# A graph attention pair with its per-head order of work changed: normalisation by bank, maxima further ahead, the q chain on GpSimd, a_src rows from bfloat16 parts, h in quarters

## The chip, the cores and the metric

One core of a Trainium2 chip runs the whole program. The metric is the device time of one execution in microseconds (us). Three runs of the kernel before took 1505.25, 1492.67 and 1501.57 us, so the median is 1501.57 us. The profile is one further execution.

## The reference

`x` is 1024 nodes by 512 features. A graph layer, a mixture of experts, a graph attention pair and a second mixture of experts each add their result to `x`. The change is in the attention pair alone. `src` and `dst` hold 17,408 edges of the same graph. For each of the two layers (8 heads, 128 channels per head in the first, 64 in the second):

```
h = (x @ W).reshape(N, heads, out_ch)
a_src = einsum('nhc,hc->nh', h, att_src);  a_dst = einsum('nhc,hc->nh', h, att_dst)
e = leaky_relu(a_src[src] + a_dst[dst], 0.2)
m = segment_max(e, dst);  ex = exp(e - m[dst]);  s = segment_sum(ex, dst)
out = segment_sum(h[src] * (ex / (s[dst] + 1e-16)), dst) + bias
```

Layer 1 is followed by relu, layer 2 by a log_softmax over its 512 features.

## The kernel before

The graph is dense in this kernel: `CT` holds, for every pair of source (partition) and destination (free axis), the logarithm of how many edges there are, and `mask` (bfloat16) a large number where there is no edge. `attend` (line 1268) runs twice, "a1" for layer 1 and "a2" (`final`) for layer 2. A **pair** is one head and one tile of 128 source nodes: 8 heads x 8 tiles = 64 pairs, numbered k, with head hd = k // 8 and tile s = k % 8. Each engine has its own in-order program and the programs meet at semaphores.

For every pair: GpSimd adds `CT` and the q row of the head (`qb`) into `am` (L1339, a ring of 4); ScalarE writes the relu of a_dst + a_src into PSUM banks 4 and 5 (L1350, one buffer, so relu of pair k+1 waits until VectorE has added pair k); VectorE adds the two (`counted`, L1438); ScalarE takes the exponential into `PT` (L1357, a ring of 4; ScalarE's order is relu k+1, then exp k); TensorE multiplies `PT` with `h`. In layer 1 this is `gather` (L1536): 8 matmuls of 129 columns (128 channels and a column of ones that gives the sum s), for 8 destination tiles in 3 PSUM banks (PER = 3 tiles a bank, NBK = 3), opened by 3 matmuls on zeros (L1532) once VectorE has emptied the banks. In layer 2 it is `columns` (L1547): two matmuls of 512 columns with the result transposed in banks 0 and 1, which ScalarE copies out once a head (`moved`, L1364, at s = 1 of the next head), TensorE turns back (`rows`, L1558, at s = 2) and VectorE divides (`normed`, at s = 4).

`normed` (L1440 to L1459) divides a head's sums. In layer 1 it comes at s = 1 of the next head and reads all three banks with one instruction; TensorE turns the result (`turned`, L1568, at s = 3 and 7) and ScalarE moves it to x2T (`out`, L1368, at s = 6 and s = 1).

The q row of a head needs the maximum of a_src over the neighbours of each node. `a_row` (L1517) has TensorE broadcast row a_src of the head to all partitions in banks 6 and 7, from the float32 tile `aTs`; `maxed` (L1422) takes 8 masked maxima on VectorE from it; `q` (L1425 to L1433) makes four instructions of 8 columns from these; SP then writes q4 to memory (L1319), waits for it, and loads it as a broadcast `qb` (L1321). The maxima of heads 0 and 1 are taken before the first pair. Those of head hd + 2 are taken in head hd, the last one and q at s = 0 of the next.

`h` comes as 16 units (`h_tile`, L1523), one per node tile and half of the heads. The 8 units of the first half are made before the first pair, the 8 of the second between gathers, by the table H_AFTER (3, 2, 2 and 1 of them in heads 0 to 3), all through bank 3; ScalarE moves them to `h` (`h_moved`, L1373) by the table H_MOVED. `turned` and `rows` use bank 3 too, so they wait for the moving of each unit in front of them.

## Time and profile before

| | |
|---|---|
| median of 3 runs | 1501.57 us (1492.67 to 1505.25) |
| profiled execution, own time | 1511.43 us, span 1509.7 us |
| TensorE matmul busy | 1096.2 us (73%) |
| VectorE busy | 950.1 us (63%) |
| ScalarE busy | 607.4 us (40%) |
| GpSimd busy | 581.9 us (39%) |
| mean granted TensorE clock | 0.844 |
| attention layer 1 | from 806.7 to 1057.6 us of the span |
| attention layer 2 | from 1057.6 to about 1350 us of the span |

A busy share is a mean over the whole program. The attention pair has to be read from its own stretch, head by head: where an engine sat idle, and what released it. In a timeline row the first number is the start in us from the span's start, the second the length, then the engine, the line, the operation, the tiles, how many records are merged, and in brackets the idle time in front of it with its releaser. A float32 matmul leaves two records, so 16 records of L1536 are one gather.

### The profile page before, as it was taken

The page shows a single profiled execution, that of the slowest core. Times are in us where ns is not written, and L with a number is a line of the kernel's source. Part 1 is how long each engine was busy: PE and PEld are TensorE (multiplying, and loading weights), DVE is VectorE, ACT ScalarE, POOL GpSimd, SP SyncE. Part 2 cuts the span into 40 slices and gives each one's busy share as a digit, 9 for nine tenths or more (in the row PEclk, how much of TensorE's full clock was granted, in tenths as well). Part 3 has the DMA queues.
Part 4 walks back from the last instruction along what each step waited for, and adds up shares of the span by engine and source line. Part 5 has one row for each costly group of instructions (what it writes and reads, how often), then busy time and mean ns, then how long its engine had stood idle before and what let it go on. Part 6 is the DMA issues. An engine that isn't in the chain of part 4 may idle for free. (4 is left out here: it accounts for less than half of the span.)

```text
span 1509.7 us, 18794 instructions
## 1 busy us (share of the span) xinstructions
PE 1096.2 (73%) x5288; PEld 754.5 (50%) x5292; DVE 950.1 (63%) x1829; ACT 607.4 (40%) x835; POOL 581.9 (39%) x493
## 2 busy tenths in 40 slices
PE   3788768952478788778607899968999876816586
PEld 1343356741467777667303477858454421205473
DVE  6466576448345566565595689994277777464355
ACT  0322343230233343443111477767046767731231
POOL 0000044403668784000330576765066667601102
PEclk9999979965678899998758899979899988865697
DMA  2000000032488999998512111110211011001795
GB/s 87 0 0 1 0 1 0 0 122 79 151 262 276 304 299 295 298 305 280 169 40 72 42 43 29 54 32 15 72 42 43 28 49 42 14 1 36 260 322 185
DMA packets 118761, 164.20 MB, mean 109 GB/s; under 512 B 26357, under 2 KB 68925, under 8 KB 118698
## 3 DMA queue, kind: packets, MB, share of 16 engines
q1 hardware_dynamic: 101722, 124.37, 26.3%
q0 software_dynamic: 5600, 18.35, 3.8%
q10 hardware_dynamic: 11376, 20.71, 3.7%
q8 instruction: 30, 0.49, 0.1%
q14 instruction: 33, 0.27, 0.1%
HBM read 133.59 MB, written 29.82 MB: 108 GB/s over the span
## 5 line engine op out<-in xcount | busy, mean ns | idle before, releaser
L1339 POOL TENSOR_TENSOR am<-CT,qb 128x1024 f32<-128x1024 f32 x128 | 300.6, 2362 | 193.2 <-DMA qb<-q_scratch 110.3
L1438 DVE TENSOR_TENSOR am<-PS,am 128x1024 f32<-128x1024 f32 x128 | 156.6, 1223 | 53.3 <-ACT PS L1350 48.6
L1350 ACT ACTIVATE PS<-adb,ab 128x1024 f32<-128x1024 f32 x128 | 143.0, 1117 | 103.2 <-DVE am L1438 102.7
L973 PE MATMUL PS<-xgT,w1r 128*128 128x128 f32 x1264 | 179.1, 303 | 2.6 <-DMA w2r<-in_L_ffn_W 2.6
L973 PEld LDWEIGHTS PS<-xgT,w1r 128*128 128x128 f32 x1264 | 172.2, 219 | 4.1 <-DMA w2r<-in_L_ffn_W 3.4
L1422 DVE CUSTOM_DVE_ANT_0 masked<-PS,mask 128x1024 f32<-128x1024 f32 x128 | 156.1, 1220 | 27.8 <-issue 26.1
L1547 PE MATMUL PS<-PT,h 128*65 128x512 f32 x256 | 136.0, 679 | 37.3 <-ACT PT L1357 19.8
L1357 ACT ACTIVATE PT<-am,as 128x1024 f32<-128x1024 f32 x128 | 145.1, 1134 | 0.7 <-DVE am L1438 0.6
L1536 PEld LDWEIGHTS PS<-h,PT 128*128 128x128 f32 x1024 | 127.9, 206 | 11.3 <-ACT PT L1357 7.5
L1055 DVE TENSOR_TENSOR w2l<-w2r,w2h 128x1024 fp32r<-128x1024 f32 x79 | 105.6, 1337 | 43.5 <-ACT w2h L1023 42.4
L1536 PE MATMUL PS<-h,PT 128*128 128x129 f32 x1024 | 128.6, 289 | 5.5 <-ACT PT L1357 5.5
L1010 ACT ACTIVATE hT<-PS,b1T 128x128 f32<-128x128 f32 x158 | 49.5, 364 | 194.4 <-PE PS L973 126.8
L964 PE MATMUL PS<-ident,xg 128*128 128x128 f32 x316 | 56.8, 309 | 87.0 <-DMA xg<-xs_scratch 86.5
L1051 DVE COPY yo<-PS 128x512 f32<-128x512 f32 x79 | 54.5, 690 | 100.8 <-PE PS L983 82.4
L335 DVE TENSOR_SCALAR oh_src<-iota,eT 128x1024 f16 x164 | 78.8, 481 | 55.8 <-PE PS L451 45.3
L1023 ACT CAST w2h<-w2r 128x1024 fp32r<-128x1024 f32 x79 | 82.5, 1045 | 59.3 <-DMA w2r<-in_L_ffn_W 45.5
L885 POOL TENSOR_TENSOR prod<-prod 128x256 f32<-128x256 f32 (+4 forms) x176 | 94.2, 535 | 13.8
L1547 PEld LDWEIGHTS PS<-PT,h 128*65 128x65 f32 x256 | 37.2, 156 | 124.0 <-issue 61.0
L964 PEld LDWEIGHTS PS<-ident,xg 128*128 128x128 f32 x316 | 39.0, 154 | 112.3 <-DMA xg<-xs_scratch 82.4
L451 PE MATMUL PS<-oh_src,oh_dst 128*128 x328 | 78.2, 386 | 22.5 <-DVE oh_dst L337 22.5
L171 PE MATMUL PS<-ident,xln 128*128 128x128 f32 x96 | 19.7, 374 | 84.6 <-DVE xln L152 83.9
L1045 DVE COPY xgT<-PS 128x512 f32<-128x512 f32 x79 | 53.9, 682 | 37.1 <-PE PS L964 37.1
(288 smaller groups left out, 1852.4 us busy)
## 6 DMA issues: line engine op xcount, KB each, us to landing
w1r<-in_L_ffn_W SPq DMA_DIRECT2D x79, 512.0 KB, 5.3
w2r<-in_L_ffn_W SPq DMA_DIRECT2D x79, 512.0 KB, 6.9
ys_scratch<-yo ACTq DMA_DIRECT2D x79, 256.0 KB, 4.9
xg<-xs_scratch SPq DMA_DIRECT2D x71, 128.0 KB, 4.6
adb<-a_scratch SPq DMA_DIRECT2D x16, 512.0 KB, 3.7
qb<-q_scratch SPq DMA_DIRECT2D x16, 512.0 KB, 4.1
wc<-in_L_gnn_W POOLq DMA_DIRECT2D x16, 256.0 KB, 5.7
xg<-xs_scratch SPq DMA_DIRECT2D x15, 256.0 KB, 5.1
```

Of the source, the lines that this page charges most:

```text
L885: pool.tensor_tensor(to, by[:, :, 0:width], by[:, :, width:2 * width], ALU.add).then_inc(s_prod, 1)
L964: mm = pe.transpose(PS[:, j % 2, k * P:(k + 1) * P], xg[:, j, k * P:(k + 1) * P], ident[:])
L973: mm = pe.matmul(PS[:, 2 + j % 2, c * P:(c + 1) * P], w1r[:, j, k, c * P:(c + 1) * P], xgT[:, j % 2, k, :], start=(k == 0), stop=(k == KD ...
L1023: act.copy(w2h[:, j % 2, :, :], w2r[:, j, :, :]).then_inc(s_wh, 1)
L1055: dve.tensor_tensor(w2l[:, j % 2, :, :], w2r[:, j, :, :], w2h[:, j % 2, :, :].bitcast(F32), ALU.subtract).then_inc(s_wl, 1)
L1339: pool.tensor_tensor(am[:, k % RING, :], CT[:, s, :], qb[:, hd % 2, :], ALU.add).then_inc(s_sum, 1)
L1350: act.activation(RELU, adb[:, hd % 2, :], ACT.Relu, bias=ab[:, s, hd:hd + 1]).then_inc(s_relu, 1)
L1357: act.activation(PT[:, k % PR, :], am[:, k % RING, :], ACT.Exp, bias=as02[:, s, hd:hd + 1], scale=1 - NEG_SLOPE).then_inc(s_exp, 1)
L1422: dve.tensor_tensor_reduce(masked[:], ASB, mask[:, t, :], 1.0, -3.0e38, ALU.subtract, ALU.max, mrow[:, hd % 2, t:t + 1]).then_inc(s_max, 1)
L1438: dve.tensor_tensor(am[:, k % RING, :], RELU, am[:, k % RING, :], ALU.add).then_inc(s_all, 1)
L1536: mm = pe.matmul(PS[:, d // PER, (d % PER) * (CH + 1):(d % PER + 1) * (CH + 1)], PT[:, (NT * hd + s) % PR, d * P:(d + 1) * P], h[:, s, hd, ...
L1547: mm = pe.matmul(PS[0:CH + 1, half, :], h[:, s, hd, :], PT[:, (NT * hd + s) % PR, half * 512:(half + 1) * 512], start=(s == 0), stop=(s == ...
```

## The change

- `normed` in layer 1 moves from s = 1 to s = 0 of the next head and divides bank by bank with three instructions, each with its own count on s_ev. `gather` loses the three zero matmuls; its first matmul into each bank starts the bank, and waits for that bank's count.
- `moved` in layer 2 goes from s = 1 to s = 0.
- q leaves VectorE. GpSimd does it in five instructions, behind the add of pair 8(hd-1) for heads from 3 on, and behind pairs 4 and 7 for heads 1 and 2. The q row of head 0 is made by TensorE (8 broadcast matmuls, `q_row`) and a copy on ScalarE, with no trip through memory.
- 13 maxima are taken before the first pair (16 before), the rest one or two behind each add; the first of head hd + 3 at s = 7 of head hd.
- `a_row` for heads from 2 on is a bfloat16 matmul over 80 rows: `aTs` is split into three bfloat16 parts in `a3` by ScalarE copies and GpSimd subtractions before the first pair. It stands in front of the gather of s = 5, three heads ahead (from head 3 on), and waits for all maxima of the head in front.
- `h`: 6 units before the first pair, 10 later (2, 2, 2, 1, 2, 1 in heads 0 to 5). A unit of the second half is now two node tiles by two heads: twice the matmuls with half the columns.
- Every gather waits for the units it reads (`h_ready`). The adb and qb rows have semaphores of their own.

```diff
-            H_AFTER = {(0, 1): 0, (0, 3): 1, (0, 5): 2, (1, 1): 3, (1, 5): 4, (2, 1): 5, (2, 5): 6, (3, 1): 7}
-            H_MOVED = {(0, 4): 0, (0, 6): 1, (1, 0): 2, (1, 4): 3, (2, 0): 4, (2, 4): 5, (3, 0): 6, (3, 4): 7}
-            MAXED = {2: (0,), 3: (1,), 4: (2,), 5: (3,), 6: (4,), 7: (5, 6)}
+            H0 = 6
+            H_AFTER = dict(zip(((0, 1), (0, 3), (1, 1), (1, 5), (2, 1), (2, 5), (3, 5), (4, 1), (4, 5), (5, 1)),
+                               range(H0, 2 * NT)))
+            H_MOVED = {(hd + (s + 3) // NT, (s + 3) % NT): i for (hd, s), i in H_AFTER.items()}
+            EARLY = 5
+            FIRST = {0: ((1, 5),), 1: ((1, 6),), 2: ((1, 7),), 3: ((2, 0), (2, 1)), 4: ((2, 2), (2, 3)),
+                     5: ((2, 4), (2, 5)), 6: ((2, 6), (2, 7)), 7: ((3, 0),)}
+            LATER = ({0: (1,), 1: (2,), 2: (3,), 3: (4,), 5: (5, 6), 6: (7,)} if final else
+                     {1: (1,), 2: (2,), 3: (3,), 4: (4, 5), 5: (6,), 6: (7,)})
+            A_ROW = {1: 2, **{8 * (hd - 3) + 5: hd for hd in range(3, HEADS)}}
+            Q_AFTER = {4: 1, 7: 2, **{NT * (hd - 1): hd for hd in range(3, HEADS)}}
...
+                    def q(hd):
+                        pool.wait_ge(s_max, NT * hd + NT)
+                        a_dst = ab[:, :, HEADS + hd:HEADS + hd + 1].rearrange("p t o -> p (t o)")
+                        link(pool.tensor_tensor(zx[:], mrow[:, hd % 2, :], a_dst, ALU.add), 4 * hd + 1)
+                        link(pool.tensor_scalar(zy[:], zx[:], 0.0, SLOPE - 1, ALU.max, ALU.mult), 4 * hd + 2)
+                        link(pool.tensor_tensor(zx[:], zx[:], zy[:], ALU.add), 4 * hd + 3)
+                        link(pool.tensor_tensor(zx[:], a_dst, zx[:], ALU.subtract), 4 * hd + 4)
+                        wait(pool, s_qrow, 16 * (hd - 2))
+                        pool.tensor_scalar(q4[:, hd % 2, :], zx[:], 1 / (SLOPE - 1), None, ALU.mult).then_inc(s_q, 1)
...
+                    pool.wait_ge(s_high, 1)
+                    pool.tensor_tensor(rest[:], aTs[:], a3[0:2 * HEADS, :], ALU.subtract).then_inc(s_rest, 1)
+                    pool.wait_ge(s_mid, 1)
+                    pool.tensor_tensor(rest[:], rest[:], mid[:], ALU.subtract).then_inc(s_last, 1)
...
+                    for i in range(2, H0 - 2):
+                        h_moved(i, i % 2)
+                    act.wait_ge(s_q0, 1)
+                    act.copy(qb[:, 0, :], PS[:, 2:4, :].rearrange("p a n -> p (a n)")).then_inc(s_q0m, 1)
...
                     relu(0)
+                    for i in range(H0 - 2, H0):
+                        h_moved(i, i % 2)
...
-                        if final and s == 1 and hd:
+                        if final and s == 0 and hd:
                             moved(hd - 1)
...
-                        if s == 0 and hd and hd + 1 < HEADS:
-                            maxed(hd + 1, NT - 1)
-                            q(hd + 1)
-                        if hd and s == (4 if final else 1):
+                        if hd and s == (4 if final else 0):
                             normed(hd - 1)
-                        if hd + 2 < HEADS:
-                            for t in MAXED.get(s, ()):
-                                maxed(hd + 2, t)
+                        for ahead, t in maxima(hd, s):
+                            maxed(ahead, t)
...
                     def a_row(hd):
                         wait(pe, s_max, NT * hd)
+                        if hd >= 2:
+                            pe.wait_ge(s_a3, 1)
+                            for half in range(2):
+                                mm = pe.matmul(PS[:, 6 + half, :], sel[0:A3, hd:hd + 1].to_broadcast([A3, P]),
+                                               a3[0:A3, half * 512:(half + 1) * 512], start=True, stop=True)
+                            mm.then_inc(s_as, 1)
+                            return
...
                     def gather(hd, s):
-                        if s == 0:
-                            wait(pe, s_ev, hd)
-                            for b in range(NBK):
-                                pe.matmul(PS[:, b, 0:PER * (CH + 1)], onesb[:], zerob[:, 0:PER * (CH + 1)],
-                                          start=True, stop=False)
+                        h_ready(hd, s)
                         pe.wait_ge(s_exp, NT * hd + s + 1)
                         for d in range(NT):
+                            if s == 0 and d % PER == 0:
+                                wait(pe, s_ev, NBK * (hd - 1) + d // PER + 1)
...
-                        if s == 0 and hd + 2 < HEADS:
-                            a_row(hd + 2)
+                        if k in A_ROW:
+                            a_row(A_ROW[k])
                         columns(hd, s) if final else gather(hd, s)
```

## Rows read from the trace of the kernel before

**Rows 1.** Head 1, layer 1, by windows: us, busy PE, PEld, DVE, ACT, POOL, PEclk, DMA.

```profile
910.00:936.00 26.00, 25.40 (x161) 19.17 (x159) 25.16 (x40) 19.14 (x21) 18.77 (x8) 1.00 0.14 42
```

**Rows 2.** TensorE's timeline in layer 1.

```profile
857.34 5.92 PE L1536 MATMUL PS<-h,PT 128*128 128x129 f32 x32 [4.75 <-ACT PT L1357]
...
870.11 3.60 PE L1523 MATMUL PS<-W1t,xT 128*128 128x512 f32 x8
...
880.55 3.73 PE L1536 MATMUL PS<-h,PT 128*128 128x129 f32 x32
...
981.50 1.98 PE L1517 MATMUL PS<-aTs,ident 16*128 16x512 f32 x4
989.25 1.15 PE L1532 MATMUL PS<-zerob,onesb 128*128 128x387 bf16 x3 [5.77 <-DVE o L1458]
...
1045.07 7.39 PE L1536 MATMUL PS<-h,PT 128*128 128x129 f32 x64
```

**Rows 3.** VectorE's timeline at the head ends of layer 1.

```profile
981.38 2.27 DVE L1429 TENSOR_TENSOR zx<-mrow,ab 128x8 f32<-128x8 f32 x1
...
986.25 1.22 DVE L1438 TENSOR_TENSOR am<-PS,am 128x1024 f32<-128x1024 f32 x1
...
987.83 1.36 DVE L1458 TENSOR_TENSOR o<-PS,rd 128x1152 f32<-128x1152 f32 x1
989.11 1.21 DVE L1438 TENSOR_TENSOR am<-PS,am 128x1024 f32<-128x1024 f32 x1
...
991.58 1.23 DVE L1438 TENSOR_TENSOR am<-PS,am 128x1024 f32<-128x1024 f32 x1
...
1001.50 1.22 DVE L1438 TENSOR_TENSOR am<-PS,am 128x1024 f32<-128x1024 f32 x1
...
1005.06 1.22 DVE L1438 TENSOR_TENSOR am<-PS,am 128x1024 f32<-128x1024 f32 x1
```

**Rows 4.** ScalarE's timeline in front of the first pairs of layer 1.

```profile
833.04 0.59 ACT L1373 COPY h<-PS 128x512 f32<-128x512 f32 x1 [2.85 <-PE PS L1523]
...
856.14 1.15 ACT L1357 ACTIVATE PT<-am,as 128x1024 f32<-128x1024 f32 x1
```

**Rows 5.** SP's timeline in layer 1, two issues of head 1.

```profile
852.57 0.37 SPq L1319 DMA_DIRECT2D q_scratch<-q  x1
862.13 0.32 SPq L1321 DMA_DIRECT2D qb<-q_scratch  x1
```

**Rows 6.** VectorE, ScalarE and TensorE by timeline, layer 2, where head 4 begins.

```profile
1221.76 1.22 DVE L1438 TENSOR_TENSOR am<-PS,am 128x1024 f32<-128x1024 f32 x1
...
1224.07 1.13 ACT L1357 ACTIVATE PT<-am,as 128x1024 f32<-128x1024 f32 x1
...
1228.20 0.99 ACT L1364 COPY a_oT<-PS 65x1024 f32<-65x1024 f32 x1
...
1236.67 0.66 PE L1558 MATMUL PS<-ident,a_oT 65*128 65x65 f32 x8
1237.16 3.60 PE L1547 MATMUL PS<-PT,h 128*65 128x512 f32 x8
```

**Rows 7.** Other places of layer 2 by timeline, TensorE and VectorE.

```profile
1243.05 7.06 PE L1547 MATMUL PS<-PT,h 128*65 128x512 f32 x12 [2.29 <-ACT PT L1357]
...
1306.65 8.14 PE L1547 MATMUL PS<-PT,h 128*65 128x512 f32 x12 [3.93 <-ACT a_oT L1364]
...
1154.38 0.17 DVE L1447 TENSOR_SCALAR dn<-PS 128x8 f32<-128x8 f32 x1 [4.39 <-PE PS L1558]
...
1315.32 0.17 DVE L1447 TENSOR_SCALAR dn<-PS 128x8 f32<-128x8 f32 x1 [3.90 <-PE PS L1558]
```

**Rows 8.** A stretch of layer 2 by windows: us, PE busy, PEclk, DMA share, GB/s.

```profile
1244.00:1247.70 3.70, 3.70 (x6) 0.54 0.00 0
```

**Rows 9.** GpSimd: line 1339 by source, and one group by form.

```profile
L1339 POOL TENSOR_TENSOR am<-CT,qb x128: 2337/2362/2397, 842.8 to 1311.2; 128x1024 f32<-128x1024 f32 x128
...
L885 POOL TENSOR_TENSOR prod<-prod 128x8 f32<-128x8 f32 x16 | 5.9, 370 | 1.3
```

More of the change, by code:

```diff
@@ L1315, in _ @@
                             sp.wait_ge(s_exp, NT * (hd - 1))
-                        sp.dma_start(adb[:, hd % 2, :], bcast(adr[HEADS + hd], N)).then_inc(s_in[hd % 2], 16)
-                        sp.wait_ge(s_q, hd + 1)
-                        with nc.allow_non_contiguous_dma(reason="one value per tile and partition"):
-                            sp.dma_start(qdr[hd].rearrange("(t p) -> p t", p=P), q4[:, hd % 2, :]).then_inc(s_qrow, 16)
-                        sp.wait_ge(s_qrow, 16 * (hd + 1))
@@ L1321, in _ @@
-                        sp.dma_start(qb[:, hd % 2, :], bcast(qdr[hd], N)).then_inc(s_in[hd % 2], 16)
-                        if final and hd == 4:
+                        sp.dma_start(adb[:, hd % 2, :], bcast(adr[HEADS + hd], N)).then_inc(s_ad[hd % 2], 16)
+                        if hd:
+                            sp.wait_ge(s_q, hd + 1)
+                            with nc.allow_non_contiguous_dma(reason="one value per tile and partition"):
+                                sp.dma_start(qdr[hd].rearrange("(t p) -> p t", p=P), q4[:, hd % 2, :]
+                                             ).then_inc(s_qrow, 16)
+                            sp.wait_ge(s_qrow, 16 * hd)
+                            sp.dma_start(qb[:, hd % 2, :], bcast(qdr[hd], N)).then_inc(s_qb[hd % 2], 16)
@@ L1554, in rows @@
                         wait(pe, s_ev, hd)
-                        wait(pe, s_hm, NT + moved)
+                        wait(pe, s_hm, moved)
                         for d in range(NT):
@@ L1569, in turned, with q_row @@
                         mm.then_inc(s_tr, 1)
+                    def q_row(hd):
+                        pe.wait_ge(s_q, hd + 1)
+                        pe.wait_ge(s_bm, 1)
+                        for t in range(NT):
+                            mm = pe.matmul(PS[:, 2 + t // 4, (t % 4) * P:(t % 4 + 1) * P],
+                                           q4[:, hd % 2, t:t + 1].to_broadcast([P, P]), ident[:], start=True, stop=True)
+                        mm.then_inc(s_q0, 1)
                     a_row(0)
                     pe.wait_ge(s_w[0], 16)
-                    for t in range(NT):
-                        wait(pe, s_hm, t - 1)
-                        h_tile(0, t, t % 2)
-                        if t == 4:
+                    for i in range(H0):
+                        wait(pe, s_hm, i - 1)
+                        h_tile(i, i % 2)
+                        if i == H0 - 3:
                             a_row(1)
+                            q_row(0)
                     pe.wait_ge(s_w[1], 16)
-                    pe.wait_ge(s_hm, NT)
+                    pe.wait_ge(s_hm, H0)
+                    pe.wait_ge(s_q0m, 1)
                     pe.wait_ge(s_ones, 1)
-                    pe.wait_ge(s_bm, 1)
                     turns = 0
@@ L1601, in _ @@
                     if final:
[L1602 removed]
+                        rows(HEADS - 1, 2 * NT)
                     else:
[L1604 to L1605 removed]
+                        turned(HEADS - 1, 0, 2 * NT)
+                        turned(HEADS - 1, 1, 2 * NT)
         phase()
```

139 lines of the change are left out of this document (97 added, 42 removed).

## The prediction, made before the changed kernel was built or run

> **What bounds the kernel now.** I read the page first. Its forty slices show no engine full throughout, so the attention pair had to be read head by head. Windows over layer 1 came next: head 1 has TensorE busy 25.40 of 26.00 us, at the full granted clock [rows 1]. Heads 0 to 2 are bound by TensorE. TensorE's timeline shows what changes later: from head 3 on it sits idle at the head's end, 5.77 us in one case, until VectorE has divided [rows 2]. VectorE's timeline says why: q starts at 981.38 and the next add comes only at 986.25, so four instructions of 8 columns took 4.87 us [rows 3]. They have SBUF tiles alone as inputs, and GpSimd's 2.36 us adds run beside them [rows 9]; adds with one side in PSUM kept 1.22 us there. In layer 2 TensorE waits instead for ScalarE's copy `moved`, and VectorE then for the rows turned back [rows 6, 7].
>
> **Prices used.** A layer-1 gather takes 3.73/2 = 1.87 us at the full clock, a unit of h 3.43, a float32 a_row about 1.95 [rows 2]. Adds follow each other every 2.48 us with one maximum between them, 3.56 us with two; an exponential ends 3.45 us after its add began (1224.07 + 1.13 - 1221.76) [rows 3, 6]. A layer-2 pair on TensorE takes 1.80 us, turning back 0.5 [rows 6]. The bfloat16 a_row has no row; between 0 and the 1.95 us of the float32 one I take 0.45, since one zero matmul of 387 bfloat16 columns took at most 1.15/3 = 0.38. Three banks divided singly have no row either: between the 1.36 us of the one instruction and three times that, I take 1.5, since the work is the same 1152 columns. A unit of second-half h in layer 2 becomes 16 matmuls of 128 columns, like two gathers: 3.74 us against 3.45.
>
> An idle gap also costs clock. After 4.75 us of idle two gathers took 5.92 instead of 3.73, 2.2 us more [rows 2]; after 2.29 us the mean granted clock of 3.7 us was 0.54, nearly all of it at the lower level of 1.2 GHz, so 3.7 x 0.46 = 1.7 us were lost [rows 7, 8]. Between 0 and 2.2 us a gap I take 1.75. The Trainium skill (TensorE: Matmul & The Clock Gate, Part 1) puts the ramp penalty at under 1% of a typical kernel's span and warns against modelling it by a count. By it the clock terms below fall away and the sum would be -19.5 us instead of -4.
>
> **Start of layer 1.** The fourth unit of h is done at 833.0 [rows 4]. Then come a_row(1) 1.95, q_row (8 matmuls of 128 columns, like a gather) 1.7 to 1.9, ScalarE's copy 1.0 and relu 1.1. Units 4 and 5 end at 843.5 and their copy at 844.1; relu and the exponential with its table load take 3.6 more, so the first gather starts at 847.7. It was 857.34 [rows 2]. The a3 copies fit in ScalarE's gaps of 2.85 us [rows 4]; without them they would cost some 3 us. Head 0 then has two units instead of three, but VectorE, which has 11 maxima left to fit in behind its adds, holds a_row(3) to about 866. Its last gather ends at 872.5, against 880.55 + 3.73 = 884.3: **-11.8**.
>
> **Heads 1 to 7 of layer 1.** Let 0 be the end of the last gather of the head before. VectorE, which has added pair 0 already, is now held at `normed` until exactly this moment; before, q and one more add covered that wait. The first bank is divided at 1.05, so gather 0 runs to 2.95. All three are done at 1.95; add 1 follows, its exponential ends at 5.4, and TensorE idles 2.5 us. Gather 1 to 7.3, unit to 10.8, gathers 2 and 3, a turn and gather 4 to 17.0, with the clock price 18.7. Adds run at 1.95, 4.4, 6.9, 9.4, 13.0, 15.4, so the head's last maximum is in at 17.9. a_row waits for it, and gather 5 behind a_row. Then 0.45, gather 5, a unit, gathers 6 and 7: 18.7 + 0.45 + 3 x 1.87 + 3.43 = 28.2. Heads 1, 2 and 4 take this. Head 3 has no early unit, so TensorE idles about 3 us in front of a_row: 17.9 + 9.5 + 1.75 = 29.2. Head 5 has no a_row and ends with its last exponential, 23.4; heads 6 and 7 with no maxima 22.3 each. The sum is 181.8. Before it was 1052.46 - 884.3 = 168.2 [rows 2]: **+13.6**. The removed zero matmuls and q are in this; their cover is gone with them.
>
> **Start of layer 2.** The same steps bring the first pair 8.4 us forward. `moved` now follows the exponential of s = 0: it begins 3.45 us after add 0, where it began 6.4 after (1228.20 - 1221.76) [rows 6]. `rows` is held by the move of the unit behind s = 1 at s = 4, and head 1 still starts at the low clock. Head 0's division comes at 1147.3 instead of 1154.4 [rows 7]: **-7.1**.
>
> **Heads 1 to 7 of layer 2.** Let 0 be the start of add 0. `moved` ends at 4.4, which delays relu 2 and so add 2 to 5.5; adds 3 and 4 start at 8.0 and 10.4. The unit behind s = 1 can be moved at 14.3 only, behind the exponential of s = 4, so `rows` ends and the division begins at 14.9 (11.7 where there is no such unit). Adds 5 and 6 start at 16.0 and 19.6, and the last maximum is in at 22.1. a_row waits for it; behind it stand 0.45, three pairs of 1.80, a unit of 3.74 and the clock, 11.5 us together, so the head's last pair ends at 33.7 and `moved` at 34.7. VectorE alone would begin the next head at 24.6 and allow `moved` to end at 29.0. The head thus takes 24.6 + 5.7 = 30.2: heads 2 and 4. Head 1, which starts behind a gap, has its first three pairs slow, 1.5 us more at the division: 31.7. Head 3 has no early unit, 3.2 less: 27.1. Head 5 has no a_row: 24.6. Head 6 has no maxima, 20.2, and starts behind a gap of 1.7: 21.7. Head 7's division stands 13.1 after its add 0, head 1's 16.4. That makes 165.5 + 13.1 - 16.4 = 162.2 between the divisions of heads 0 and 6, against 1315.3 - 1154.4 = 160.9: **+1.3**. From there to the end nothing changes; the bias load now follows the last qb and lands long before the log_softmax needs it.
>
> **GpSimd and SP.** The five instructions of q have between 0 and 5 x 2.36 = 11.8 us, the length of five whole adds; the nearest row has 8 columns in 0.37 us [rows 9], so I take 2 us with the waits between them. q(hd) stands between pairs 0 and 1 of head hd - 1 in GpSimd's queue, and begins when the last maximum is in. From there add 1 of the next head leaves it 9 us in layer 1's heads with a late unit and 5 in head 5. Layer 2 leaves 2 to 3 us before add 1 itself is late, but in heads 1 to 4 add 2 waits for `moved` far longer. So it costs nothing; at the upper end it would cost 3 to 7 us in most heads. q4's way through memory takes 9.56 us [rows 5], then the load, for which I allow 4; it stands behind adb in SP's queue, and the tightest case, head 7 of layer 2, has 2.5 us to spare. Nothing for it either.
>
> **Sum.** -11.8 + 13.6 - 7.1 + 1.3 = -4.0 us. The profiled execution took 1511.43 us with a span of 1509.7, so it would come to 1507.4. It lies 9.9 above the median; I apply the difference to the median: 1501.57 - 4 = **1497.6 us**.
>
> **Rivals.** *Clock stays up (faster).* The gap at a head's start is cut in two by gather 0, and the gap in front of a_row can come out shorter than 2.29 us. Then 1.75 goes four times in layer 1 where 0.7 (three heads) and 1.75 (head 3) was exposed (-4), and in layer 2 four times behind a_row and three times in front of the division (-11.4): 1501.57 - 19.5 = 1482. For it: head 1 of layer 1 never left the full clock [rows 1], and by the sum above TensorE stays busy 23 of a head's 28 us. Against it: 2.29 us was enough [rows 7, 8]. Chance 0.26.
>
> *TensorE starts cold twice a head (slower).* Place: heads 1 to 4 of both layers, at the division and behind a_row, where now two gaps stand instead of one. In one row three pairs took 8.14 instead of 5.4 us after a gap [rows 7], 2.7 each. Twice 2.7 less the 1.75 counted is 3.65 a head, 8 heads, +29: 1527. It decides once a head's two gaps cost over 4.2 us, where the time passes 1% above the median. Against it: VectorE's waits hide part of the first one. Chance 0.12. The Trainium skill (TensorE: Matmul & The Clock Gate, HAM oscillation) describes a loop in which every turn's gap brings the clock down anew; by it the time is this rival's.
>
> *The wait at `normed` is not there (faster).* If VectorE were never held, heads would run at its own 21.9 and the change would win over 25 us, 1475. Against it: the last gather ends 1.9 us behind its exponential, and the add of pair 0 ends before that. Chance 0.05. *q or its row comes late*, or the change acts nowhere: 0.02, same range as the forecast.
>
> **The numbers.** The forecast has 0.55 with its own range of 1488 to 1507, from the bounds of the clock and of the three-bank division (8 heads x 1 us). To hold 8 in 10 the range takes in the first rival and leaves out the second: 1477 to 1513. One per cent, about what a measurement tells from no change, is 15 us. Faster by over 1% (below 1486.6): 0.29, from the two fast rivals and a tail. Slower by over 1%: 0.12. Within: 0.59.
>
> **What would show it.** Right: the first gather of layer 1 near 848; VectorE idle in front of `normed` in layer 1 for 1 to 6 us, released by TensorE; heads 1 to 4 of layer 1 at 27 to 29 us and longer than before; heads 6 and 7 at 22; TensorE waiting at a_row for a maximum; clock 0.50 behind it. Wrong: heads of layer 1 under 25 us, no wait of VectorE for the last gather, GpSimd's q over 5 us, or qb as the releaser of adds.

## The result: 0.7% faster, inside the forecast

| | before | changed |
|---|---|---|
| median | 1499.22 us (20 runs, 1489.08 to 1505.25) | 1488.14 us (20 runs, 1474.25 to 1495.73) |
| profiled execution, own time | 1511.43 us | 1485.29 us |
| span | 1509.7 us | 1483.0 us |
| ratio of the times | | 0.993, interval 0.9904 to 0.9955 |

The change gains 11.1 us where I had forecast 4.0 with 1477 to 1513 around it. It is less than the 1% that I had set as the bound of "the same", but outside the measurement's own uncertainty. The median of the kernel before is now 1499.22 us over 20 runs, where the forecast started from 1501.57 over 3.

The two profiled spans lie 26.7 us apart, more than the medians do; the profiled execution of the kernel before was slower than each of its 20 timed runs. To see which part belongs to the change I cut each span at three places that both traces have: the first matmul of a_src and a_dst of layer 1, that of layer 2, and the first statistics of the normalisation behind the attention. All times in this table are differences of such starts.

| us | before | changed | difference |
|---|---|---|---|
| ahead of the attention (code unchanged) | 806.79 | 791.84 | -15.0 |
| layer 1 | 250.88 | 252.25 | +1.4 |
| of it, to the end of head 0's last gather | 77.5 | 67.0 | -10.5 |
| of it, heads 1 to 7 | 168.2 | 179.0 | +10.8 |
| layer 2 | 294.29 | 279.47 | -14.8 |
| of it, to the division of head 0 | 96.7 | 85.6 | -11.1 |
| of it, divisions of heads 0 to 6 | 160.95 | 158.09 | -2.9 |
| behind the attention (code unchanged) | 157.74 | 159.44 | +1.7 |

The attention and what follows it differ by 11.8 us, about the medians' 11.1. The 15 us ahead of it lie in code that neither kernel changes. In the eleven other profiles of this study that stretch took 788 to 802 us, so one profile says little about it, and I count none of it for the change. The same spread bounds every reading below: identical code of layer 2 took 279.5, 279.7 and 276.3 us in three kernels, identical code of layer 1 252.3 and 255.4. The starts of the layers hold in all of them: 65.4 to 68.9 us for head 0 of layer 1 in the eight kernels that share the changed code there (77.5 and 78.1 with the old code), 83.9 to 88.5 us in layer 2 (96.7 and 97.6).

### The profile page after: what moved, and what is told of

It is laid out like the page before. It is cut to its first block and busy times, and to the rows that moved or that the text cites. A ratio compares the mean times of both kernels' runs of the same rounds, so it can differ in the third digit from the quotient of the medians.

```text
span 1483.0 us, 19362 instructions
## 1 busy us (share of the span) xinstructions
PE 1057.4 (71%) x5468; PEld 743.3 (50%) x5468; DVE 908.0 (61%) x1781; ACT 614.4 (41%) x845; POOL 609.9 (41%) x587
## 5 line engine op out<-in xcount | busy, mean ns | idle before, releaser
L973 PE MATMUL PS<-xgT,w1r 128*128 128x128 f32 x1264 | 165.1, 287 | 3.4 <-DVE xgT L1045 1.8
L973 PEld LDWEIGHTS PS<-xgT,w1r 128*128 128x128 f32 x1264 | 157.3, 203 | 6.3 <-issue 3.0
L1647 PE MATMUL PS<-PT,h 128*65 128x512 f32 x256 | 125.6, 623 | 23.9 <-ACT PT L1427 14.1
L964 PE MATMUL PS<-ident,xg 128*128 128x128 f32 x316 | 53.1, 293 | 80.0 <-DMA xg<-xs_scratch 79.8
L451 PE MATMUL PS<-oh_src,oh_dst 128*128 x328 | 78.9, 389 | 22.0 <-DVE oh_dst L337 21.9
L964 PEld LDWEIGHTS PS<-ident,xg 128*128 128x128 f32 x316 | 35.7, 145 | 107.9 <-DMA xg<-xs_scratch 87.7
L1647 PEld LDWEIGHTS PS<-PT,h 128*65 128x65 f32 x256 | 33.5, 142 | 97.6 <-issue 80.8
L1178 POOL DMA_INDIRECT yb<-ys_scratch,r_posi x16 | 16.4, 1023 | 142.7 <-POOLq L1085 138.2
```

Source lines behind the costliest of these rows:

```text
L964: mm = pe.transpose(PS[:, j % 2, k * P:(k + 1) * P], xg[:, j, k * P:(k + 1) * P], ident[:])
L973: mm = pe.matmul(PS[:, 2 + j % 2, c * P:(c + 1) * P], w1r[:, j, k, c * P:(c + 1) * P], xgT[:, j % 2, k, :], start=(k == 0), stop=(k == KD ...
L1647: mm = pe.matmul(PS[0:CH + 1, half, :], h[:, s, hd, :], PT[:, (NT * hd + s) % PR, half * 512:(half + 1) * 512], start=(s == 0), stop=(s == ...
```

## The profile after

The head of the page of the changed kernel: busy time and share of each engine, then the costliest groups of instructions, with their idle time in front and its releaser.

```profile
PE 1057.4 (71%) x5468; PEld 743.3 (50%) x5468; DVE 908.0 (61%) x1781; ACT 614.4 (41%) x845; POOL 609.9 (41%) x587
...
L1407 POOL TENSOR_TENSOR am<-CT,qb 128x1024 f32<-128x1024 f32 x128 | 299.3, 2363 | 61.5 <-ACT PT L1427 39.5
L1520 DVE TENSOR_TENSOR am<-PS,am 128x1024 f32<-128x1024 f32 x128 | 156.6, 1223 | 77.2 <-ACT PS L1420 67.7
```

VectorE lost 42 us of work and TensorE 39 us, and the time moved by 11. That is what a busy share can't tell. Now stretches of layer 1 by windows, from division to division: first head 1 of the kernel before, then heads 1 and 2 of the changed kernel; then, in each of the two heads, what follows the gap ahead of the gather of s = 1; the last window lies in layer 2 behind an a_row. The columns are those of [rows 1].

```profile
884.32:909.23 24.91, 24.91 (x160) 19.35 (x161) 24.07 (x40) 17.21 (x18) 18.79 (x8) 1.00 0.13 43
...
858.80:886.00 27.20, 22.70 (x169) 21.39 (x169) 20.78 (x37) 19.95 (x20) 25.16 (x16) 1.00 0.15 40
886.00:914.10 28.10, 24.67 (x173) 22.94 (x172) 20.78 (x37) 19.49 (x20) 20.15 (x14) 0.94 0.15 39
...
864.29:868.00 3.71, 3.71 (x25) 3.50 (x26) 3.61 (x8) 3.27 (x4) 3.71 (x3) 1.00 0.03 4
891.93:898.80 6.87, 6.87 (x32) 6.11 (x33) 6.45 (x14) 6.29 (x7) 6.47 (x3) 0.75 0.26 76
...
1137.60:1141.20 3.60, 3.60 (x6) 1.23 (x5) 3.44 (x7) 2.96 (x4) 3.43 (x5) 0.50 0.02 5
```

In head 1 of the kernel before TensorE was busy for all of 24.91 us. Here it is busy for 22.70 of 27.20: head 1 has less work for it and takes longer. The window of [rows 1], which I called head 1, is head 2 by the divisions (909.23 to 935.47 us); it went from 25.40 of 26.00 us to 24.67 of 28.10. TensorE's timeline shows where it stands, first around the division of head 0, then in head 3 of layer 1:

```profile
854.75 4.07 PE L1634 MATMUL PS<-h,PT 128*128 128x129 f32 x35
860.01 2.02 PE L1634 MATMUL PS<-h,PT 128*128 128x129 f32 x16 [1.20 <-DVE o L1545]
864.29 2.02 PE L1634 MATMUL PS<-h,PT 128*128 128x129 f32 x16 [2.26 <-ACT PT L1427]
...
932.15 0.60 PE L1602 MATMUL PS<-a,sel 80*128 80x512 bf16 x2 [2.86 <-DVE mrow L1514]
932.60 1.95 PE L1634 MATMUL PS<-h,PT 128*128 128x129 f32 x16
934.38 3.62 PE L1619 MATMUL PS<-W1t,xT 128*128 128x256 f32 x16
```

VectorE's timeline at the same division, in order. It waits for the last gather, divides three banks, and only then comes the add of pair 1:

```profile
856.38 1.23 DVE L1520 TENSOR_TENSOR am<-PS,am 128x1024 f32<-128x1024 f32 x1 [1.59 <-POOL am L1407]
858.86 0.17 DVE L1529 TENSOR_SCALAR dn<-PS 128x9 f32<-128x9 f32 x1 [1.25 <-PE PS L1634]
859.06 0.22 DVE L1531 RECIPROCAL rd<-dn 128x9 f32<-128x9 f32 x1
859.31 1.49 DVE L1545 TENSOR_TENSOR o<-PS,rd 128x384 f32<-128x384 f32 x3
860.71 1.22 DVE L1520 TENSOR_TENSOR am<-PS,am 128x1024 f32<-128x1024 f32 x1
```

This wait of VectorE is in all eight heads of layer 1; its group of instructions puts 31.6 us on TensorE's gather (3.74 of them behind head 7, where nothing is held up by it), and 19.3 us on the turned rows of layer 2:

```profile
L1529 DVE TENSOR_SCALAR dn<-PS 128x9 f32<-128x9 f32 (+1 forms) x16 | 2.6, 166 | 50.9 <-PE PS L1634 31.6 <-PE PS L1658 19.3
```

In layer 2, head 1, TensorE waits for the maximum, falls to the lower of its two clock levels (0.50 granted, 1.2 GHz, window 1137.60 above), and stands again for `moved`. The last two rows are the a_row of head 3, where the pair behind a wait of 2.98 us ran at its full speed:

```profile
1136.76 1.04 PE L1602 MATMUL PS<-a,sel 80*128 80x512 bf16 x2 [3.63 <-DVE mrow L1514]
1137.59 3.62 PE L1647 MATMUL PS<-PT,h 128*65 128x512 f32 x4
1141.00 4.47 PE L1619 MATMUL PS<-W2t,x2T 128*128 128x128 f32 x32
1145.30 3.60 PE L1647 MATMUL PS<-PT,h 128*65 128x512 f32 x8
1150.00 1.93 PE L1647 MATMUL PS<-PT,h 128*65 128x512 f32 x4 [1.10 <-ACT a_oT L1434]
...
1195.48 0.60 PE L1602 MATMUL PS<-a,sel 80*128 80x512 bf16 x2 [2.98 <-DVE mrow L1514]
1195.92 1.88 PE L1647 MATMUL PS<-PT,h 128*65 128x512 f32 x4
```

q, which took VectorE 4.87 us in [rows 3] (two instructions of 2.27 us and two of 0.17), takes GpSimd 1.5 us from its first to its last instruction, here for head 0 and in every head behind it:

```profile
813.87 0.21 POOL L1379 TENSOR_TENSOR zx<-mrow,ab 128x8 f32<-128x8 f32 x1 [0.70 <-DVE mrow L1514]
814.17 0.27 POOL L1380 TENSOR_SCALAR zy<-zx 128x8 f32<-128x8 f32 x1
814.53 0.20 POOL L1381 TENSOR_TENSOR zx<-zx,zy 128x8 f32<-128x8 f32 x1
814.81 0.21 POOL L1382 TENSOR_TENSOR zx<-ab,zx 128x8 f32<-128x8 f32 x1
815.10 0.25 POOL L1384 TENSOR_SCALAR q<-zx 128x8 f32<-128x8 f32 x1
```

## The experiments

Each ran beside the kernel before, whose own median was 1503.58 us for e1 to e4, 1505.29 for e5 to e8 and 1507.84 for e9 to e11; so runs of different sets are compared by their ratios. Lengths of layers and heads come from one profile each and are read as in the table above; a head of layer 1 goes from division to division, a head of layer 2 from one `moved` to the next. In three groups: what each part of the change is worth, what holds the heads back, and what comes of mending it.

### The parts

**e4: q back on VectorE**, behind the last maximum, with its old four instructions.

```diff
-                        if k in Q_AFTER:
-                            q(Q_AFTER[k])
...
                             maxed(ahead, t)
+                            if t == NT - 1:
+                                q(ahead)
```

> The changed kernel with q of every head on VectorE again, four instructions right behind the head's last maximum (slot s = 6), and nothing of it on GpSimd. Theory (VectorE does not bound the changed heads, it waits for TensorE at the division): the 0.8 to 5 us of q shorten that wait in layer 1 and nothing else in heads 0 to 4; a few us are lost in head 5 and layer 2, together 0 to 10 us. Rival (taking q off VectorE is where the gain came from): 4.9 us in each of six heads of layer 1 and up to 2 in those of layer 2, 30 us or more.

Measured: 1517.3 us, ratio to before 1.0107 (1.0013 to 1.02). Layer 1 took 271.1 us, layer 2 290.3. Heads 1, 2 and 4 of layer 1 stayed within 0.4 us (27.6, 28.1, 27.7 against 27.2, 28.1, 27.7), as the theory had it. But head 0 grew by 9.8 us in layer 1 and 10.3 in layer 2, head 3 by 2.4, head 5 by 5.7. The total of 29.7 us is about the rival's (30 or more), but it sits elsewhere than the rival had it: where no other wait covers VectorE. Head 0 of layer 1 has two such chains, 3.9 us at 837.35 and 7.0 us at 855.58. VectorE's timeline of the second, and GpSimd's adds beside it:

```profile
855.58 0.17 DVE L1506 TENSOR_TENSOR zx<-mrow,ab 128x8 f32<-128x8 f32 x1
855.78 2.25 DVE L1507 SCALAR_TENSOR_TENSOR zx<-zx 128x8 f32<-128x8 f32 x1
858.06 2.27 DVE L1508 TENSOR_TENSOR zx<-ab,zx 128x8 f32<-128x8 f32 x1
860.36 2.27 DVE L1510 TENSOR_SCALAR q<-zx 128x8 f32<-128x8 f32 x1
862.54 1.21 DVE L1515 TENSOR_TENSOR am<-PS,am 128x1024 f32<-128x1024 f32 x1
...
855.66 6.94 POOL L1394 TENSOR_TENSOR am<-CT,qb 128x1024 f32<-128x1024 f32 x3 [8.56 <-DMA qb<-q_scratch]
```

Eight columns for 0.17 us, begun 0.08 us ahead of GpSimd's first add; then for 2.25 to 2.27 us three times. GpSimd's three adds run without a break from 855.66 to 862.60, and the three slow instructions end at 858.03, 860.33 and 862.63, as the adds do. Put back on VectorE alone, q costs more than twice what the whole change gained in the attention (13.5 us).

**e3: all a_row float32**, the bfloat16 parts still computed.

```diff
-                        if hd >= 2:
+                        if hd >= HEADS:
                             pe.wait_ge(s_a3, 1)
```

> The changed kernel with the a_src rows of all heads made from the float32 tile, as before; the splitting into three bfloat16 parts is still done, nothing reads it. Theory: a_row stands in the chain of TensorE in heads 0 to 4 of both layers, so 1.95 - 0.45 = 1.5 us come back up to ten times, 10 to 15 us in all, shared evenly. Rival (hidden): TensorE's row is off the chain, under 3 us.

Measured: 1515.9 us, ratio 1.0097 (1.0065 to 1.0129). Layer 1 took 17.5 us more, layer 2 13.1, two to three times the 10 to 15 us expected for both. Head 0 of layer 1 lost 6.7 us and head 3 6.2; heads 1, 2 and 4 lost 1.6, 1.6 and 1.3, as much as the two prices differ. TensorE's timeline has the a_row at 1.98 us (that of bfloat16 starts 0.44 us ahead of its successor), and, behind the next division, a gather that ran at the lower clock:

```profile
879.87 1.98 PE L1607 MATMUL PS<-aTs,ident 16*128 16x512 f32 x4 [1.05 <-DVE mrow L1514]
...
896.74 3.45 PE L1634 MATMUL PS<-h,PT 128*128 128x129 f32 x16 [2.25 <-ACT PT L1427]
```

The gap was there in the changed kernel as well (2.26 us), where that gather took 2.02 us in head 1 and 2.46 in head 2. So the parts save about 1.5 us in heads 1, 2 and 4, and more in heads 0 and 3; that the clock and the start of the layer make the rest is my reading, not separated by a run.

**e8: all eight units of the first half ahead of the first gather.**

```diff
-            H0 = 6
+            H0 = 8
```

> The changed kernel with H0 = 8: the whole first half of h stands ahead of the first gather, as before the change, and eight quarters instead of ten units stand among the pairs; the a_row of head 1 and the row q of head 0 come two units later, in both layers. Theory (a unit moved is a unit saved elsewhere at the same price): the first gather of a layer 6.5 to 7.5 us later (two units of 3.5), and the heads that lose a unit 3.5 to 4 us shorter each, so that each layer stays within 2 us of the changed kernel's (252.3 and 279.5). Rival (units among the pairs of heads 0 and 1 lie beside ScalarE's exponentials, which set the pace there, and cost nothing): each layer 5 to 7 us longer, the time 10 to 14 us more than the changed kernel's.

Measured: 1490.58 us, ratio 0.9913 (0.9877 to 0.9948). The first gather of layer 1 came 49.75 us behind the layer's start, not 42.9: +6.9. Head 4, which lost its late unit, became 3.4 us shorter; head 5, which lost its early one, not at all. Layer 1 +3.3, layer 2 -3.3 (the theory had allowed 2 each, the rival had 5 to 7 in each), nothing in the sum. The shift of two units is worth nothing by itself within the spread, and the rival is out.

**e6: one division instead of three.**

```diff
+                        elif True:
+                            dve.tensor_tensor(dst, O[:, :, :, 0:CH], scale, ALU.mult).then_inc(s_ev, NBK)
```

> The changed kernel, but the division of a head of layer 1 is one VectorE instruction over all banks, still at s = 0 of the next head, and not one a bank. Theory: bank by bank brings nothing, since the gather of s = 1 waits for its exponential whether the gather of s = 0 began earlier or not: layer 1 252 to 254 us (252.3 in the changed kernel). Rival (each bank's release starts TensorE earlier, and that is kept): the gather of s = 0 begins about 0.9 us later in each of seven heads, layer 1 257 to 260. Third way (one instruction instead of three is cheaper for VectorE, which is what the last maximum waits for): layer 1 248 to 251. Layer 2 as in the changed kernel, 278 to 281, in each.

Measured: 1488.34 us, ratio 0.9888 (0.9851 to 0.9925), layer 1 252.4 us as in the changed kernel. Heads 1 to 7 took 27.2, 27.3, 27.3, 27.3, 23.8, 22.7 and 21.8, head 0 1.9 us more than in the changed kernel. The division bank by bank is worth nothing where it stands: the gather of s = 1 waits for its exponential, and takes back what the gather of s = 0 gained. Layer 2, whose code is the same, ended at 276.3; that is the spread named above.

**e7: `moved` ahead of the pair of s = 0, in the kernel before.**

```diff
-                        if final and s == 1 and hd:
+                        if final and s == 0 and hd:
                             moved(hd - 1)
```

> The kernel before with one edit: in layer 2 ScalarE moves the output columns of a head out of their bank ahead of the pair of s = 0 of the next head, and not ahead of that of s = 1. Theory (the move holds TensorE's columns of s = 0 in every head, and that was the larger part of what the change gave in layer 2): 1.5 to 3 us a head over seven heads, layer 2 274 to 284 us instead of 294.3. Rival (the move is hidden behind the a_row and its maximum, and layer 2 gained by its start alone): layer 2 292 to 296. Layer 1 unchanged, 249 to 252, in both.

Measured: 1497.01 us, ratio 0.9951 (0.9915 to 0.9986). Layer 2 took 286.1 us instead of 294.3, between the two expectations. The six heads between divisions took 151.6 us, 9.4 less than before. The changed kernel has this move too, and 158.1 us. So about 6.5 us of it are lost again to the rest of the change in these heads. Its start of layer 2, 97.6 us, shows that the 11.1 us at the start come from elsewhere.

### What holds the heads back

**e1: the division of layer 1 back behind the add of s = 1.**

```diff
-                        if hd and s == (4 if final else 0):
+                        if hd and s == (4 if final else 1):
```

> The changed kernel with layer 1's division back at s = 1 of the next head (still bank by bank). Layer 1 takes 252.3 us in the changed kernel's trace, from its first matmul to that of layer 2. Theory (VectorE held at the division drains the pipeline): the exponential of pair 1 is then ready before the last gather ends, the 2.26 us idle of TensorE in front of gather 1 goes in every head, heads 5 to 7 become about 2.2 us shorter each and heads 1 to 4 about 3 us each, so layer 1 takes 232 to 240 us and the program about 15 us less. Rival (the early division frees the banks and is itself the gain): layer 1 gets 3 to 8 us longer. Rival (TensorE's own work bounds heads 1 to 4): only heads 5 to 7 gain, 5 to 7 us in all.

Measured: 1475.26 us, ratio 0.9824 (0.9754 to 0.9895); layer 1 244.1 us. Heads 5, 6 and 7 gained 1.0, 2.3 and 2.7 us. Heads 1 to 4 took 25.9, 27.6, 27.6 and 27.6: all but the first nearly what they took before. At 8.2 us the rival is nearer than the theory. The gap of 2.26 us at the head's start is gone. In heads 2 to 4 TensorE stands in front of the a_row instead, for 2.0 to 2.9 us, and in head 2 the gather behind it runs at the lower clock:

```profile
898.16 1.95 PE L1634 MATMUL PS<-h,PT 128*128 128x129 f32 x16
902.11 0.60 PE L1602 MATMUL PS<-a,sel 80*128 80x512 bf16 x2 [2.00 <-DVE mrow L1514]
902.55 3.49 PE L1634 MATMUL PS<-h,PT 128*128 128x129 f32 x16
905.84 3.77 PE L1619 MATMUL PS<-W1t,xT 128*128 128x256 f32 x16
```

So in these heads the a_row waits for the last maximum, and the unit of h that could fill the wait stands behind it.

**e2: that unit one pair earlier, in layer 2.**

```diff
+            LATE = 4 if final else 5
-            H_AFTER = ... (1, 5), ... (2, 5), (3, 5), ... (4, 5) ...
+            H_AFTER = ... (1, LATE), ... (2, LATE), (3, LATE), ... (4, LATE) ...
```

> The changed kernel with the late unit of h of a head placed behind the pair of s = 4 instead of s = 5, in layer 2 alone, so that it stands in front of a_row instead of behind it. Layer 2 takes 279.5 us in the changed kernel's trace (first matmul to the first statistics of the next layernorm), heads 1, 2 and 4 about 31 us each. Theory (a_row waits 3 to 3.6 us for a maximum with TensorE idle, and the unit behind it makes the copy of the sums late): the unit fills the wait, the last pair ends before its copy is due, heads 1, 2 and 4 take 25 to 26 us and head 3 about 23, so layer 2 takes 258 to 266 us. Rival (the chain of adds and exponentials bounds the heads anyway): layer 2 stays within 3 us. Rival (the clock alone costs it): 1 to 2 us in each of four heads, 4 to 7 us.

Measured: 1472.42 us, ratio 0.9791 (0.9707 to 0.9874); layer 2 257.6 us, 21.9 less. That is 0.4 us below the theory's lower bound. Between divisions the heads took 25.0, 21.2, 25.2, 24.6, 21.2 and 20.4. TensorE's timeline of head 1: the unit fills what was 3.63 us of idle time, the a_row waits for nothing, and the three pairs behind it run at the full clock.

```profile
1140.32 3.73 PE L1620 MATMUL PS<-W2t,x2T 128*128 128x128 f32 x32
1144.11 0.61 PE L1603 MATMUL PS<-a,sel 80*128 80x512 bf16 x2
1144.55 5.32 PE L1648 MATMUL PS<-PT,h 128*65 128x512 f32 x12
```

### Both layers together

**e5: three edits.** The division behind s = 1, the late unit behind s = 4 in both layers (`LATE` stands in `H_AFTER` as in e2), and ScalarE's move of a head's turned first half at s = 4.

```diff
+            LATE = 4
-                        if not final and s == 6 and hd:
+                        if not final and s == 4 and hd:
                             out(hd - 1, 0)
-                        if hd and s == (4 if final else 0):
+                        if hd and s == (4 if final else 1):
```

> The changed kernel with three edits: the division of a head of layer 1 again behind the pairs of s = 1, the late unit of h of heads 1 to 4 behind the gather of s = 4 in both layers, and the first half of the turning of a head's output behind s = 4 of the next head. Theory: the two single gains add up and the a_row of layer 1 loses its 2 us wait, since the last maximum of a head is no longer behind late adds: layer 1 232 to 240 us (252.3 in the changed kernel, 244.1 with the first edit alone), layer 2 256 to 260 (279.5), the whole attention 488 to 500 instead of 531.7; the time 1442 to 1460 us. Rival (TensorE's own chain of matmuls sets heads 1 to 4, wherever the units stand): layer 1 stays at 243 to 247, the time 1462 to 1472. Second rival (the earlier turning waits for the division's banks and holds the queue of TensorE): layer 1 250 or more.

Measured: 1447.95 us, ratio 0.9637 (0.9582 to 0.9693). Layer 1 took 231.3 us, layer 2 261.8, 493.1 together; the sum and the time lie inside the theory's bounds, layer 1 is 0.7 us below its own and layer 2 1.8 above. Heads 1 to 4 of layer 1 took 23.7, 23.8, 22.9 and 23.8 us. This version beats both kernels: 57 us below the kernel before in its comparison. Head 2 by windows, and the wait at the division, which was 31.6 us on the gathers and is 5.5 (3.74 of it behind head 7, as before):

```profile
880.35:904.13 23.78, 22.93 (x172) 21.50 (x171) 20.77 (x37) 19.49 (x21) 19.84 (x14) 1.00 0.16 46
```

```profile
L1530 DVE TENSOR_SCALAR dn<-PS 128x9 f32<-128x9 f32 (+1 forms) x16 | 2.6, 164 | 24.7 <-PE PS L1659 19.1 <-PE PS L1635 5.5
```

**e9: e5 without the earlier turning.**

```diff
-                        if not final and s == 4 and hd:
+                        if not final and s == 6 and hd:
                             out(hd - 1, 0)
```

> The best version so far without the earlier turning: division of layer 1 behind s = 1, late units behind s = 4 in both layers, first half of the turning behind s = 6 as in the changed kernel. Theory (the late unit between the pairs of s = 4 and 5 fills the wait for the last maximum, so that the a_row finds it there and no clock is lost, and the turning behind s = 6 is nearly as good): layer 1 231 to 236 us (231.3 with the earlier turning, 244.1 without either). Rival (the earlier turning gave the larger part, since ScalarE's move of the turned half stood ahead of the pair that the a_row frees): 238 to 243. Layer 2 258 to 263 in both.

Measured: 1473.61 us, ratio 0.9759 (0.9711 to 0.9806); layer 1 259.3 us. That is 28.0 us worse than e5 and 15.2 worse than e1, which neither side had. Heads 1 to 4 took 30.2 to 30.7 us, heads 5 to 7 as in e1. TensorE's timeline in head 2:

```profile
909.39 1.95 PE L1635 MATMUL PS<-h,PT 128*128 128x129 f32 x16
915.06 6.46 PE L1620 MATMUL PS<-W1t,xT 128*128 128x256 f32 x16 [3.72 <-ACT x2T L1439]
921.36 0.60 PE L1603 MATMUL PS<-a,sel 80*128 80x512 bf16 x2
```

The unit and the turned half share bank 3. The turning puts its half there at s = 3, and ScalarE takes it out only behind the exponential of s = 6. A unit at s = 4 waits for that, 3.72 us, and then runs at the lower clock, 6.46 us instead of 3.62, with the a_row behind it.

**e10: the units alone, in both layers.** The changed kernel with `LATE = 4` in `H_AFTER`.

```diff
+            LATE = 4
```

> The changed kernel with one edit: the late unit of h of heads 1 to 4 behind s = 4 in both layers; the division stays behind s = 0. Theory (the two edits are needed together: with the division at s = 0 the gather of s = 1 still waits 2.3 us for its exponential, and TensorE still falls to the lower clock there): layer 1 247 to 252 us (252.3 in the changed kernel, 244.1 with the division's edit alone, 231.3 with both and the earlier turning). Rival (the late unit alone makes the gain of layer 1): 236 to 244. Layer 2 256 to 262 in both.

Measured: 1482.5 us, ratio 0.9811 (0.9763 to 0.986); layer 1 264.6 us, 12.4 more than the changed kernel. Both sides missed, for e9's reason: here too the unit waits (2.95 us) for `out`. Layer 2 took 261.3 us.

```profile
916.74 5.38 PE L1620 MATMUL PS<-W1t,xT 128*128 128x256 f32 x16 [2.95 <-ACT x2T L1439]
```

**e11: e5 with the division at s = 0.**

```diff
-                        if hd and s == (4 if final else 1):
+                        if hd and s == (4 if final else 0):
```

> The best version so far with the division of layer 1 at s = 0, as the changed kernel has it. Theory (the place of the division is what holds heads 1 to 7 of layer 1 back, by the gap ahead of the gather of s = 1 and the clock behind it, whatever the units do): layer 1 245 to 251 us, against 231.3 with the division at s = 1; heads 5 to 7 22 to 24 us each. Rival (with the units behind s = 4 the gap ahead of the gather of s = 1 is filled by nothing but costs nothing, since the adds set the pace): layer 1 231 to 238. Layer 2 258 to 263 in both.

Measured: 1470.49 us, ratio 0.9759 (0.9709 to 0.981); layer 1 247.1 us against 231.3, as the theory had it, every head from 1 to 7 longer by 1.5 to 3.9 us. That is the division's place alone, 15.8 us by the profiles and 18 by the two ratios, and the gap ahead of the gather of s = 1 is back:

```profile
889.16 2.02 PE L1635 MATMUL PS<-h,PT 128*128 128x129 f32 x16 [1.17 <-DVE o L1546]
893.44 2.02 PE L1635 MATMUL PS<-h,PT 128*128 128x129 f32 x16 [2.25 <-ACT PT L1428]
```

Layer 1 in the six kernels that vary these three places, in us:

| division | late unit | first half out | layer 1 |
|---|---|---|---|
| s = 0 | s = 5 | s = 6 | 252.3 (changed kernel) |
| s = 1 | s = 5 | s = 6 | 244.1 (e1) |
| s = 0 | s = 4 | s = 6 | 264.6 (e10) |
| s = 1 | s = 4 | s = 6 | 259.3 (e9) |
| s = 0 | s = 4 | s = 4 | 247.1 (e11) |
| s = 1 | s = 4 | s = 4 | 231.3 (e5) |

The unit's earlier place did only harm as long as the bank was not free for it. With the earlier move beside it, the two together gave 12.8 us (e1 to e5). The earlier move with the unit left at s = 5 was not run, so its own share of the 12.8 us is open.

The whole runs bear these lengths out. What both layers gained on the kernel before, by the profiles, lies inside the interval of the time's ratio for the changed kernel and nine of the experiments. In e9 and e10 it does not: 28.5 us against 36.3 by the ratio (29.3 to 43.6), and 19.3 against 28.5 (21.1 to 35.7). The harm of 15.2 and 12.4 us that their profiles show may thus be some us too large; its sign is in four heads of each. What no run took back: the new order of the maxima, the a_row's new place, and the q row of head 0 on TensorE.

## Why the prediction was right, step by step

**The frame.** That the change wins at the start of each layer and gives it back in the heads of layer 1 held: -10.5 and +10.8 against -11.8 and +13.6. In layer 2 -11.1 and -2.9 stand against -7.1 and +1.3. Three of the four terms came out lower than I had put them, one higher, and the sum is -13.7 against -4.0 (-13.5 over both layers by their ends). So the sign and the frame were worked out, but the forecast was a small difference of terms of 19 and 15 us, and its range of 36 us would have held no change at all as well. The measured median stands at the edge of the forecast's own range (1488 to 1507). [rows 1] shows head 2 and not head 1; head 1 was at the full clock too, so the argument stands. Two sums in the heads of layer 2 are off by 0.1 and 0.2 us, which moves nothing.

**Start of layer 1.** The first gather came 42.9 us behind the layer's start, where it had been 50.6: 7.7 us earlier, not 9.6; e8 puts 6.9 of them on the two units. Head 0 then gained 2.8 more, not 2.2. e4, e3 and e8 take back one part at a time: q on GpSimd 9.8 us of head 0, the bfloat16 parts 6.7, the two units fewer ahead of the first gather 7.0. These don't add up to the 10.5: each part taken back alone leaves the others their full weight, and what they cost together was not tried. My step had no term for q there; that its chains on VectorE would cost 3.9 and 7.0 us in head 0, beside the adds that run there, I had not worked out.

**Heads 1 to 7 of layer 1.** The mechanism was the one described, to the place: VectorE held at `normed` until the last gather (1.25 to 5.82 us in heads 0 to 4), three banks done in 1.5, a gap of 2.26 us (2.5 forecast) ahead of the gather of s = 1, the a_row waiting for the last maximum in head 3 (2.86, forecast 3). Head 1 took 27.2 us and heads 2, 3 and 4 28.1, 27.5 and 27.7, for 28.2, 28.2, 29.2 and 28.2; heads 5 to 7 23.8, 22.8 and 21.9, for 23.4, 22.3 and 22.3. What was off is the clock term, by where it falls and not by its size. After the same 2.26 us, head 1's unit took 3.62 us at a granted 1.00 and head 2's 4.90, at 0.75 over 6.87 us. Behind this gap heads 2, 3 and 4 lost 1.7 to 1.8 us each, about the 1.75 assumed, and head 1 nothing; and in head 3 the 2.86 us in front of the a_row cost no clock: the gather behind it took 1.95. Heads 1 and 3 are 1.0 and 1.7 us below their forecasts, which is the 2.8 us between forecast and result. e11 and e1 confirm that the division's place is what costs. e6 confirms that dividing bank by bank is not what pays.

**Start of layer 2.** Here the step was off by 4.0 us: 85.6 us to head 0's division and not 89.6. The parts named in it are there. I had carried over 8.4 us from layer 1's start and left the rest to a first unit and a wait for `moved`. In the eight kernels with this code the start took 85.9 us on average, 11.3 less than the 97.1 of the two with the old. It took 83.9 to 85.6 us in five of them and 88.0 to 88.5 in three, so up to 3 us of the 4.0 are spread. About 1.3 us of the difference to before is in the first product of the layer (15.29 us instead of 16.57), whose code did not change; with the new code it took 16.6 as well (e1, e5). And 10.3 us come back when q goes back to VectorE (e4). What the remainder is made of was not separated.

**Heads of layer 2.** The structure held: `moved` ahead of the exponential of s = 1 (1.10 us of TensorE's wait at 1150.00), the a_row waiting for the last maximum (3.63), and low clock behind it (0.50) in heads 1, 2 and 4. From one `moved` to the next the heads took 31.4, 31.0, 24.9, 29.7, 24.6, 20.4 and 19.3 us, for forecasts of 31.7, 30.2, 27.1, 30.2, 24.6 and 21.7 between the divisions of heads 0 to 6. Head 3 and head 6 are the difference. Head 3 had the clock's price behind its a_row, and the pair there took 1.88 us after a wait of 2.98; head 6 had it at its start, and did not lose it. So what was off is again where the clock falls, -2.2 and -1.3 us, 3.5 of the 4.2 us between forecast and result. That e2 takes 21.9 us out by moving one unit shows how much of these heads was that wait and its clock.

**Rivals.** *Clock stays up* had -19.5 us and 0.26. It happened in part: in head 1 and at the a_row of head 3 of layer 1 and in heads 3 and 6 of layer 2, not behind the first gap of heads 2 to 4 of layer 1 nor behind the a_row of heads 1, 2 and 4 of layer 2. Over both layers the mean granted clock was 0.93, where it had been 0.88. The Trainium skill (TensorE: Matmul & The Clock Gate, Part 1) puts the ramp at under 1% of a span; here single groups of matmuls took 3.62 us behind the a_row of layer 2 where they take 1.88 at full clock, and e2, which took those waits away with the clock they cost, gained 21.9 of 1483.0 us, 1.5%. The trace does not part the waits from the clock in it, so the rule is neither shown nor refuted as a share of the span. The measured -11.1 us lies about midway between the -19.5 without clock terms and the -4.0 with them. *Cold twice a head*, with +29, did not occur as a pattern. Head 1 of layer 2 alone was slow behind both gaps (two pairs in 5.34 us where they take 3.60, then one in 3.62), and e9 is what it looks like in layer 1: one more wait of 3.72 us in a head, behind which a unit takes 6.46 us, and heads of 30.5 us. *The wait at normed is not there*: it is, 31.6 us of it.

**GpSimd and SP.** I had taken 2 us for q and its waits and costed them at nothing; the chain is 1.5 us. `qb` as the releaser of adds was one of my signs of being wrong: two adds of GpSimd waited for it, 0.51 and 1.42 us, where twelve had in the kernel before, up to 3.48 us, besides the first of each layer. In e5, with shorter heads, eleven wait again, up to 2.17 us; in head 2 of its layer 1 TensorE is busy for 22.93 of 23.78 us, so it does not bound that head.

## What to carry to other kernels

When a wait moves, look at what is queued behind it on the engine that waits: the division moved from s = 1 to s = 0 cost 15.8 us in a schedule that was otherwise free, by holding the add of the next pair for the last gather. A piece of filler work (here a unit of h) belongs in front of the wait that it can fill, but only when the bank that it writes is free by then; the unit's edit without the bank's lost 15.2 us, both together won 12.8 (the bank's without the unit's was not tried). So try the schedule's places in combinations, not one by one.

## What the runs showed of the hardware

- A VectorE instruction of 8 columns with its operands in SBUF took 0.17 us or 2.25 us, depending on whether a GpSimd add of 2.36 us had begun, and ended with that add; the adds with one side in PSUM kept 1.22 us beside the same GpSimd adds. The Trainium skill (SBUF — State Buffer, SBUF: two separate sides) describes a lock on a port pair held for a whole instruction. The 2.25 us of e4 agree with it. In e4 this was covered in heads 1, 2 and 4 of layer 1; in head 0, without cover, q cost 9.8 us.
- TensorE's clock after a gap is not a function of the gap's length in these traces. After 2.26 us of idle time, what followed ran at a granted 1.00 in one head and 0.75 in the next. After 2.00 us (e1) a gather took 3.49 us, and after 2.86 us (changed kernel, head 3) 1.95. A term for it should be a range from zero up, for each gap.
- The same code in two profiles differed by up to 4.5 us in a stretch of 260 (layer 2 in the five kernels with the late unit behind s = 4), and by up to 18.4 us in one of 800. A single profile of each kernel doesn't settle a question of a few us; the heads, each repeating the same pattern, do.
- What stays open: why the stretch ahead of the attention was longest in the two profiles with the old attention code (806.8 and 801.9 us, against 788 to 799). The medians don't need it for the changed kernel, and no run separated it.
